# An LSTM step in an adaLN feed-forward kernel: the f32 product for h goes from VectorE to GpSimd

## What is computed

```python
def step(carry, xw_t):                      # 64 times, one after another
    prev_h, prev_c = carry
    a = xw_t + prev_h @ Wh                  # Wh: 256 x 1024
    i, f, o = sigmoid(a[:, :256]), sigmoid(a[:, 256:512]), sigmoid(a[:, 512:768])
    g = tanh(a[:, 768:])
    next_c = f * prev_c + i * g
    next_h = o * tanh(next_c)
    return (next_h, next_c), next_h
...
h = s0 * conn_dense(k0, concat([hs, -hs]))  # 512 -> 1024
h = s1 * conn_dense(k1, relu(h) * 2)        # 1024 -> 1024
out = x + s2 * conn_dense(k2, relu(h) * 2)  # 1024 -> 256
```

## Time and profile before

| | |
|---|---|
| median of 3 runs | 277.18 us (277.06 to 278.49) |
| span of the profiled execution | 276.0 us, first to last instruction |
| what lies around the span | 277.18 - 276.0 = 1.2 us |
| granted TensorE clock | 1.000 |
| PE busy | 272.2 us, 99% of the span |
| DVE busy | 203.5 us, 74% |
| ACT busy | 158.0 us, 57% |
| POOL busy | 2.2 us, 1% |

### The profile page before, as it was taken

How to read it: one execution, slowest core, us unless ns; L and a number is a source line. 1 busy time by engine, 2 the same in 40 slices (tenths; PEclk the granted TensorE clock), 3 DMA queues, 4 the chain that set the end, 5 groups by cost and what they waited for, 6 DMA issues and landing times.

```text
span 276.0 us, 8792 instructions
## 1 busy us (share of the span) xinstructions
PE 272.2 (99%) x3616; PEld 224.0 (81%) x3616; DVE 203.5 (74%) x751; ACT 158.0 (57%) x482; POOL 2.2 (1%) x10
## 2 busy tenths in 40 slices
PE   8999999999999999999999999999999999999996
PEld 5887888888999998999999999999999996444443
DVE  3778888878888888888888888888887876532213
ACT  5689787878566656655555566555665554411100
POOL 0200000000000000000000000000000000000000
DMA  6970000000000000000000000000000000010002
GB/s 221 362 298 1 4 2 0 2 4 2 2 2 0 5 21 21 2 2 4 21 23 2 1 21 21 2 2 23 22 3 0 21 23 2 0 38 2 0 0 76
DMA packets 5191, 8.72 MB, mean 32 GB/s; under 512 B 672, under 2 KB 3488, under 8 KB 5024
## 3 DMA queue, kind: packets, MB, share of 16 engines
q1 hardware_dynamic: 4864, 7.64, 7.8%
q10 hardware_dynamic: 288, 0.52, 0.5%
HBM read 6.07 MB, written 2.10 MB: 30 GB/s over the span
## 4 chain that ended last, share of the span: by engine, by line
PE 97%; DMA 1%; DVE 0%; DVEq 0%; issue 0%
PE WK L465 50%; PE WK L448 14%; PE G L427 11%; PE ACC L481 10%; PE G L418 9%; DMA x<-in_x 1%; PE G L448 1%; PE ACC L448 1%; PE G L481 0%; DVE xs L715 0%; DVE x L662 0%; DVEq L237 0%
## 5 line engine op out<-in xcount | busy, mean ns | idle before, releaser
L465 PE MATMUL WK<-h,k 128*128 128x256 f16 (+1 forms) x992 | 124.2, 276 | 0.0
L465 PEld LDWEIGHTS WK<-h,k 128*128 128x128 fp8e5 x992 | 94.2, 98 | 13.4
L609 ACT ACTIVATE tT<-aT 128x128 f32<-128x128 f32 x126 | 39.0, 310 | 56.4 <-DVE aT L759 55.2
L655 DVE SCALAR_TENSOR_TENSOR h<-WK,h 128x256 f16<-128x256 f32 (+1 forms) x105 | 42.6, 439 | 24.7 <-ACT h L574 24.7
L759 DVE TENSOR_REDUCE aT<-G 128x128 f32<-128x256 f32 x128 | 48.1, 417 | 7.7 <-PE G L427 6.1
L574 ACT ACTIVATE h<-WK 128x256 f16<-128x256 f32 (+1 forms) x104 | 36.3, 387 | 28.8 <-PE WK L465 28.8
L556 ACT ACTIVATE G<-xw 128x256 f32<-128x256 f32 x126 | 46.6, 370 | 0.0
L448 PE MATMUL WK<-xs,wxs 128*128 128x512 f32 x168 | 42.5, 400 | 0.0
L427 PE MATMUL G<-h,w 128*128 128x64 f16 x1008 | 39.5, 192 | 0.0
L418 PEld LDWEIGHTS G<-h,w 128*128 128x128 f16 x1008 | 32.9, 96 | 5.8 <-DVE h L776 4.4
L448 PEld LDWEIGHTS WK<-xs,wxs 128*128 128x128 f32 x168 | 30.4, 188 | 5.9
(11 more groups left out here) (66 smaller groups left out, 132.8 us busy)
## 6 DMA issues: line engine op xcount, KB each, us to landing
x<-in_x SPq DMA_DIRECT2D x3, 512.0 KB, 7.8
out_y<-x SPq DMA_DIRECT2D x12, 128.0 KB, 1.8
xw<-in_wh SPq DMA_DIRECT2D x4, 256.0 KB, 4.8
k<-in_k SPq DMA_DIRECT2D x1, 1024.0 KB, 9.6
x<-in_x ACTq DMA_DIRECT2D x2, 256.0 KB, 3.8
xw<-in_wx SPq DMA_DIRECT2D x4, 128.0 KB, 3.9
xw<-in_wx SPq DMA_DIRECT2D x2, 256.0 KB, 5.1
k<-in_k SPq DMA_DIRECT2D x1, 512.0 KB, 6.9
```

What stands on the lines that cost most here:

```text
L465: ins = eng.matmul(layer_src(tile), w, rhs, start=a == 0, stop=last)
L609: eng.activation(tT[:, B * j0:B * j1], aT[:, j0:j1].rearrange("p j b -> p (j b)"), ACT.Tanh, scale=half_gain0 if t == 0 else half_gain).th ...
L655: eng.scalar_tensor_tensor(layer_dst(tile, 1), layer_src(tile), 0.0, layer_dst(tile, 0), ALU.max, ALU.subtract).then_inc(lo_made[tile[0]])
```

## The change

In each step GpSimd forms the f32 product into `h32`; VectorE forms the f16 product as before, and the subtraction on VectorE now waits for both. Three more waits make it free of races: ACT's tanh into `tC` and DVE's write of `oP` wait for GpSimd's product of the step before, and GpSimd waits for the subtraction two steps back before it overwrites a half of `h32`.

```diff
@@ scalar, step t
                 e.wait_ge(c_made, t + 1)
+                e.wait_ge(h32_made, t)
                 eng.activation(tC[:, :, :].rearrange("p j b -> p (j b)"), cD[:, :], ACT.Tanh, scale=0.5).then_inc(c_tanh)
@@ vector, step t
                 e.wait_ge(tanhed[1], t + 1)
+                e.wait_ge(h32_made, t)
                 eng.tensor_scalar(oP[:, :, :].rearrange("p j b -> p (j b)"), to, HS / 2, HS / 2, ALU.mult,
                                   ALU.add).then_inc(o_made)
                 e.wait_ge(c_tanh, t + 1)
                 e.wait_ge(o_made, t + 1)
                 eng.tensor_tensor(h16[:, t, :, 0], oP[:, :, :], tC[:, :, :], ALU.mult).then_inc(hh_made)
-                eng.tensor_tensor(h32[:, t % 2], oP[:, :, :], tC[:, :, :], ALU.mult).then_inc(h32_made)
+                e.wait_ge(hh_made, t + 1)
                 e.wait_ge(h32_made, t + 1)
                 eng.tensor_tensor(h16[:, t, :, 1], h32[:, t % 2], h16[:, t, :, 0], ALU.subtract).then_inc(hl_made)
@@ gpsimd, after its casts
+            for t in range(T):
+                eng.wait_ge(c_tanh, t + 1)
+                eng.wait_ge(o_made, t + 1)
+                if t >= 2:
+                    eng.wait_ge(hl_made, t - 1)
+                eng.tensor_tensor(h32[:, t % 2], oP[:, :, :], tC[:, :, :], ALU.mult).then_inc(h32_made)
```

## The result

The changed kernel takes 281.54 us (median of 4 runs, 281.04 to 281.71), the kernel before 277.46 (4 runs): a ratio of 1.0138, interval 1.0113 to 1.0164. The forecast was 279.6, slower; the loss is 4.1 us where 2.4 were forecast. The time lies inside the stated range (276.9 to 287) and 0.1 us above the forecast's own part of it (278.6 to 281.4). The profiled run of the changed kernel is the fastest of its four (281.04), with a span of 279.2 us.

A forecast was written before the change was run, and what follows sets the result against it. PE was taken to bound the kernel, its slack nearly covering a later low part; added stalls of 1.65 us in late and 0.79 in early steps, 2.4 in all, on 277.18 gave 279.6 us, range 276.9 to 287.

The forecast's parts named there:

- What bounds the kernel: PE bounds plain steps, 3.27 or 3.38 us against 3.06 for the recurrence; a faster handover gives at most 0.45 us.
- GpSimd's product, T = 0.45: GpSimd's product ends 0.45 us behind the tanh into tC: held until 0.25, takes 0.35, 0.15 of it already passed.
- Rival 3: GpSimd's product runs whole behind VectorE's high part, ending at 0.60: +9.2 us, 286.4 us; chance 0.23.
- Rival 4: GpSimd gets in first and holds VectorE's high part until 0.43: +13.5 us, 290.7 us; chance 0.05.
- The signal and the separate wait, 0.07: Between GpSimd's product and the subtraction: 0.05 us for the signal plus 0.02 for a separate wait that ends last.
- x: How much later than before the low part of h ends in each step; forecast 0.10 us.
- What x costs: PE's added stalls from the later low part: 1.65 us in late steps plus 0.79 in early ones, 2.4 us.
- the walk: Sum over the 63 later steps with constants from the trace, giving time lost per low-part delay: 2.4 us for 0.10.
- What costs nothing: Added waits on old products cost nothing; GpSimd's set-up before its first product at 22 us is hidden up to 8 us.
- rival 1: Not slower: GpSimd is done by 0.41 us and PE's slack covers the delay; 277.1 to 278.6 us; chance 0.33.

The follow-up runs named there:

- run 4: Kernel before with the f32 product left out, the subtraction taking tC instead (low part of h not right): 277.9 us, ratio 1.0005.
- run 7: Changed kernel, but GpSimd starts its product only when VectorE's high part is made: 292.58 us, ratio 1.0536.
- run 3: Kernel before with two added waits, tanh into tC for h32_made and the subtraction for hh_made, placed first: 278.47 us, ratio 1.0027.
- run 8: Kernel before with the two added waits of run 3, but the subtraction's two waits in the other order: 277.71 us, ratio 1.0001.
- run 2: Changed kernel with the subtraction's two waits in the other order, so it carries the wait for GpSimd itself: 279.25 us, ratio 1.0055.
- run 5: Changed kernel with step 0's f32 product back on VectorE and GpSimd's loop beginning at step 1: 280.1 us, ratio 1.0097.
- run 6: Changed kernel with step 0's product on VectorE and the subtraction's two waits in the other order: 278.32 us, ratio 1.0021.
- run 1: Changed kernel with one extra GpSimd product of zeros into a scratch tile ahead of GpSimd's loop: 282.53 us, ratio 1.0162.

## Why the prediction was right in its direction, and where its size was off

**What bounds the kernel**: right. PE's steps kept their 3.27 and 3.38 us wherever the low part was early enough, and run 4 shows that VectorE's product had next to nothing to give back: 0.05 us of the stretch, where the prediction's bound was 0.45.

**GpSimd's product, T = 0.45**: measured 0.43, by another sum. It starts at 0.07 to 0.08 and not at 0.10, and takes 0.36. The prediction had 0.35 for its size and a hold by VectorE until 0.25, of which 0.15 were covered; that this gave nearly the measured end is partly luck. Alone it takes 0.32 (run 7) and the hold costs 0.04. The reading of the earlier trace rows as a wait for the other's end was too strict: by the records the product began 0.05 behind the high part and ran 0.36 us, where a whole wait for the other's end and 0.32 behind it would have made that 0.49. Rival 3, and with it the rule that the prediction took from the Trainium skill ("SBUF — State Buffer", section "Who interferes with whom"), did not happen for these two instructions; the measurement decides. Rival 4 did not either: the high part starts at 0.03 as before (but for step 61, late in both kernels).

**The signal and the separate wait, 0.07**: measured 0.10. Here the term for the separate wait was mis-sized. It was put at 0.02, between nothing and 0.05; runs 3 and 8 give 0.07, above the range. GpSimd's signal itself, put at 0.05, takes 0.03 (run 2). The errors nearly met in the sum: x = 0.11 where 0.10 was forecast. That is luck, and the parts tell another story than the prediction did. From run 5 to run 6 only the order of the two waits changes, and the stretch falls by 2.23 us; what is left of the change is 0.49.

**What x costs**: the walk puts x = 0.11 at 2.8 us. The tight steps of the changed kernel cost 2.32. For x = 0.07 it has 1.5 and run 3 shows 1.07. For x = 0.04 it has about 0.8 (at 0.045) and run 6 shows 0.3 beside its first product. It is 0.4 to 0.5 too high each time. For the large x = 0.33 it has 13.9 without the first step and run 7 shows 14.0, with step 51's late start in it, so there it is nearly right. The likely reading is some slack in the tight steps that its constants leave out and a large x uses up; no run shows where.

**"What costs nothing"**: this is the step that failed. The time until GpSimd's first product was said to be hidden as long as it took no more than 8 us, and the sum had nothing for it. No product of GpSimd started in less than 8.4 us behind the casts in any run where one was asked for, and the first step paid 0.90 us. With the 0.35 of step 51, where VectorE itself started late, that is the difference between the forecast and the measurement of the stretch: 2.4 forecast, and 2.32 + 0.90 + 0.35 = 3.57 measured. That the tight steps came to 2.32, so near 2.4, is luck as well: x was a little larger than forecast and the walk 0.4 to 0.5 too high. VectorE's busy time fell by 10.8 us and not by 13.9: the prediction added up the products' own times, of which a part overlaps the instructions beside them. Nothing hung on it. The medians differ by 4.08. In runs 2, 3, 5, 6 and 7, too, the difference of the medians and that of the stretches, which come from one profiled execution, lie up to 0.6 us apart in either direction.

**Not slower** (rival 1) would have needed T under 0.41. With the waits in the right order and step 0 on VectorE it nearly came true (1.0021), with T still 0.43.

No version beat the kernel before, and run 4 says why: with the whole product gone the time is the same. The loss itself is accounted for by what takes it away: 0.85 us of stretch go with step 0's product back on VectorE (run 5), 2.23 more with the order of the waits (run 6), and 0.49 are left.

## What to carry to other kernels

Before moving work off an engine, take it away altogether in one run: if the time stays, no other engine's version can win. When an instruction waits for two things, see which of the two waits it carries itself, and let that be the one that is fulfilled last. Before blaming a producer for a late start, compare the time of its signal with the start: in run 5 the signal was on time. An engine that needs a set-up instruction for a new kind of work may be late for its first call (here by 8.4 to 9.6 us behind its last work); give it the second step.

## What the runs showed that was not expected

- A separate wait that is fulfilled last makes VectorE start 0.07 us later each time; one fulfilled early costs nothing (runs 3 and 8, 0.10 against 0.03, everything else equal).
- GpSimd had no product ready for 8.4 to 9.6 us behind its casts, whether it was asked at 14 or at 22 us (changed kernel, runs 1, 2 and 7). First asked at 24.7 us, it was on time (run 5).
- A GpSimd product of 128x64 from two f32 tiles takes 0.32 us alone and 0.36 beside a VectorE product of the same two tiles, which itself stays at 0.22.
- After PE had idled 2.4 us in the run with the extra product, the granted clock was 0.50 in the next 2.5 us; after an idle time of 0.8 us in the changed kernel, and of 1.5 in run 7, it stayed at 1.00.
- Now and then a VectorE instruction starts 0.1 to 0.5 us late though all it waits for is there. All 17 such places in the ten traces are multiples of 64 in the count of VectorE's records.
